# Expert units ordered by tile count, with programs that prepare an equal successor and loop on themselves

## The reference, cut to what matters

```python
_, top2 = jax.lax.top_k(probs, 2)                     # two experts of four for each token
for e in range(e_total):
    member = (top2 == e).any(-1)
    order = jnp.argsort((~member).astype(jnp.int32), axis=-1, stable=True)
    xg = jnp.take_along_axis(x, order[..., None], axis=1)
    q = (xg @ wq[e] + bq[e]).reshape(b, s, h, hd)      # k and v alike
    att = jnp.einsum('bqhd,bkhd->bhqk', q, k) * sm_scale
    att = jnp.where(validg[:, None, None, :], att, -1000000000.0)
    att = jax.nn.softmax(att, axis=-1)
    y = jnp.einsum('bhqk,bkhd->bqhd', att, v).reshape(b, s, d)
    y = y @ wo[e] + bo[e]
    out = out.at[bidx, order].add(wg[..., None] * y)
```

## Time and profile before

| | us |
|---|---|
| median of 3 runs | 4405.09 |
| lowest, highest | 4398.52, 4405.25 |
| the profiled execution | 4440.01 |
| its span, first to last instruction | 4438.2 |
| PE busy | 3516.6 (79%) |
| DVE busy | 2407.3 (54%) |
| ACT busy | 2102.3 (47%) |
| POOL busy | 892.9 (20%) |

### The profile page before, as it was taken

One profiled execution on the slowest core, in us unless ns is written; L12 is line 12 of the kernel. 1 busy time (PEld: TensorE's weight loads), 2 busy tenths in 40 slices (PEclk: granted clock), 3 DMA queues, 4 the chain that ended last, 5 costly groups with the idle time before them and its releaser, 6 DMA issues.

```text
span 4438.2 us, 58078 instructions
## 1 busy us (share of the span) xinstructions
PE 3516.6 (79%) x21592; PEld 1672.6 (38%) x21593; DVE 2407.3 (54%) x3490; ACT 2102.3 (47%) x4547; POOL 892.9 (20%) x686
## 2 busy tenths in 40 slices
PE   4998989757779777797777977779279979788795
PEld 2444435332333333333333333332134435344574
DVE  3664656534366443664436644365276797875523
ACT  1664656425346553464534745347135545454121
POOL 1132422220110002100021000200233423110274
PEclk8998999869789997998989989889679989899898
DMA  4544435330431204312043121420342414123488
GB/s 137 167 147 125 134 105 169 94 79 20 110 91 33 65 20 110 89 33 65 20 115 84 33 66 32 113 73 12 100 116 84 122 55 123 38 61 100 107 202 225
DMA packets 329702, 407.57 MB, mean 92 GB/s; under 512 B 43992, under 2 KB 292120, under 8 KB 321163
## 3 DMA queue, kind: packets, MB, share of 16 engines
q1 hardware_dynamic: 277148, 346.89, 27.7%
q0 software_dynamic: 18432, 35.67, 3.4%
q10 hardware_dynamic: 33664, 19.53, 2.0%
HBM read 234.31 MB, written 158.14 MB: 88 GB/s over the span
## 4 chain that ended last, share of the span: by engine, by line
PE 54%; DVE 21%; issue 8%; DMA 5%; ACT 5%; POOL 3%; ACTq 2%; SPq 2%; another core or an unknown queue 1%; POOLq 0%; DVEq 0%
PE PSUM L768 13%; DVE M L997 13%; PE PSUM L728 10%; PE PSUM L746 10%; PE PSUM L673 6%; PE PSUM L790 3%; PE PSUM L709 2%; ACT P L938 2%; DVE best L1321 2%; DVE XR L1324 2%; ACTq L550 1%; PE PSUM L776 1%; PE PSUM L587 1%; PE PSUM L731 1%
## 5 line engine op out<-in xcount | busy, mean ns | idle before, releaser
L997 DVE TENSOR_REDUCE M<-PSUM 128x1 f32<-128x768 f32 (+7 forms) x1710 | 1715.2, 1037 | 1276.1 <-PE PSUM L728 778.1
L938 ACT ACTIVATE P<-PSUM 128x512 f32<-128x512 f32 (+2 forms) x3520 | 1577.8, 503 | 877.0 <-PE PSUM L746 524.6
L728 PE MATMUL PSUM<-KS,QS 99*128 99x512 bf16 (+3 forms) x3596 | 956.9, 349 | 410.8 <-issue 204.6
L746 PE MATMUL PSUM<-QS,KS 101*128 101x512 bf16 (+2 forms) x3520 | 1077.8, 344 | 108.4 <-ACT P L938 67.7
L768 PE MATMUL PSUM<-P,VA 128*17 128x512 f32 (+3 forms) x7040 | 779.8, 520 | 1.8 <-ACT P L938 0.9
L746 PEld LDWEIGHTS PSUM<-QS,KS 101*128 101x128 bf16 x3520 | 330.5, 99 | 858.8 <-ACT P L938 484.6
L728 PEld LDWEIGHTS PSUM<-KS,QS 99*128 99x128 bf16 x3596 | 312.1, 100 | 853.7 <-DVE M L997 373.9
L639 POOL TENSOR_TENSOR QF<-QF,PH 128x1024 f32<-128x1024 f32 (+2 forms) x98 | 160.3, 1635 | 2115.2 <-ACT PH L893 2077.8
L673 PE MATMUL PSUM<-XT,W 128*128 128x512 f32 (+2 forms) x656 | 313.5, 606 | 7.3 <-ACT P L938 3.8
L768 PEld LDWEIGHTS PSUM<-P,VA 128*17 128x17 f32 x7040 | 135.9, 97 | 239.3 <-issue 203.4
L731 PE MATMUL PSUM<-identb,maskB 128*128 128x128 bf16 x1024 | 218.3, 228 | 0.0
(11 more groups left out here) (189 smaller groups left out, 3121.6 us busy)
## 6 DMA issues: line engine op xcount, KB each, us to landing
qk_d<-PH SPq DMA_DIRECT2D x156, 256.0 KB
xg_d<-GX SPq DMA_DIRECT2D x19, 1152.0 KB, 11.1
yg_d<-GX SPq DMA_DIRECT2D x17, 1152.0 KB
XF<-xg_d SPq DMA_DIRECT2D x18, 1024.0 KB
VA<-n_L_ffn_expert_gate_up_w SPq DMA_DIRECT2D x64, 256.0 KB, 5.8
QS<-qk_d SPq DMA_DIRECT2D x42, 384.0 KB, 5.4
KS<-qk_d SPq DMA_DIRECT2D x42, 384.0 KB, 4.8
QS<-qk_d SPq DMA_DIRECT2D x42, 256.0 KB, 5.8
```

What stands on the lines that cost most here:

```text
L728: mm = e.matmul(slot_heads(s, hb)[:, x, a:b], QS[0:KA, g, h + x, 128 * qt:128 * qt + 128], KS[0:KA, g, h + x, a:b], start=True, stop=not d ...
L746: mm = e.matmul(s[:, 0:q1 - q0], KS[0:KB, g, j, 128 * kt:128 * kt + 128], QS[0:KB, g, j, q0:q1], start=True, stop=not diag, skip_group_che ...
L938: e.activation(P[:, m % NP, 0:q1 - q0], s[:, 0:q1 - q0], ACT.Exp, scale=ly.scale).then_inc(S["act_p"], 1)
L997: e.tensor_reduce(m[:, qt, h:h + hb], v[:, :, 0:kn], AX.X, ALU.max).then_inc(S["dve_a"], 1)
```

## The change

Unit 0 stays first. Units 1 to 15 are sorted on DVE by falling tile count (`order_units`: two rounds of `max` and a `match_replace` on the score 32 x tiles - u), which gives `key` and a new list `sequence` of unit numbers. A program reads from `sequence` which unit it is (u), which it prepares (nu) and whose rows it loads (nu of nu). There are 16 programs: for the first unit one of each nt that prepares at 8 tiles (kinds 1 to 8), for the others one of each nt that prepares at nt tiles (kinds 9 to 16). `key` holds the tile count of unit 0, then 8 + tiles. The register `kind` is loaded at a program's start; at its end the program compares it, and where it is its own kind it goes through a `meet` block of its own (`again`) back to its start. The rows of the second unit are loaded by the first unit's program, no longer in `l0`. The core of the diff:

```diff
-                "bk": [("dve_x", 6)],
+                "bk": [("dve_x", 15)],
-        ev += [(13.0, ("nx", B)), (13.05, ("nv", B)), (13.1, ("fr", B)), (16.1, ("nr", B))]
+        ev += [(13.0, ("nx", B)), (13.05, ("nv", B)), (13.1, ("fr", B))]
...
+    if layer.first:
+        ev.append((-2.0, ("nr", 2)))
...
+        def order_units(e, w, before):
+            later = slice(1, B * E0)
...
+            e.tensor_scalar(count, count, 1.0, 32.0, ALU.max, ALU.mult).then_inc(x, 1)
+            e.tensor_tensor(score, count[:, later], sequencef[:, later], ALU.subtract).then_inc(x, 1)
+            e.max(top[:, 0:8], score).then_inc(x, 1)
+            e.match_replace(left, top[:, 0:8], score, NEG).then_inc(x, 1)
+            e.max(top[:, 8:16], left).then_inc(x, 1)
...
+            e.tensor_scalar(keyf[:, later], tiles, float(NT), None, ALU.add).then_inc(x, 1)
+            e.scalar_tensor_tensor(sequencef[:, later], tiles, 32.0, top[:, 0:n], ALU.mult, ALU.subtract)
...
+                    if i == 3:
+                        w.wait_ge("pe_a", "xt", 2, O.layer.of(2).nch - 1, 1)
+                        e.sem_clear(S["ahead_rows"])
+                    e.dma_start(XF[:, :, :], x_rows(v["block"] if i == 3 else v["block1"]))
...
-        units = {3 * nt + a: unit_order(Unit(nt, PADS[a])) for nt in range(1, NT + 1) for a in range(3)}
+        units = {nt: unit_order(Unit(nt, FIRST, True)) for nt in range(1, NT + 1)}
+        units.update({NT + nt: unit_order(Unit(nt, nt, False)) for nt in range(1, NT + 1)})
...
+            e.dma_start(sequencef[:, :], d["c_iota"][:, 0:B * E0 + 2]).then_inc(S["setup"], 16)
...
+            kinds = [NT + nt for nt in range(NT, 0, -1)] + list(range(NT, 0, -1))
+            def names():
+                if name not in ("sp", "act"):
+                    return None
+                for k, reg in enumerate((this, after, third)):
+                    e.reg_load(reg, sequence[0:1, bass.ds(position() + k, 1)])
...
             with nc.body(label + "tests", valid_engines=on):
-                e.br_cmp(at, B * E0, label + "end", label + "key", "IS_EQ")
-            with nc.body(label + "key", valid_engines=on):
-                kind = e.value_load(key[0:1, bass.ds(unit(), 1)], min_val=kinds[0], max_val=last_kind)
-                e.br(label + f"test{kinds[0]}")
+                e.br_cmp(at, B * E0, label + "end", label + f"test{kinds[0]}", "IS_EQ")
...
                 with nc.body(label + f"program{k}", valid_engines=on):
                     hint = e.mark_branch_hint_location()
-                    u = unit()
-                    section(units[k], {"u": u, "ex": u % E0, "nu": u + 1, ...
+                    v = names()
+                    nc.regs_alu(at, at, 1, op=ALU.add)
+                    e.reg_load(kind, key[0:1, bass.ds(nc.snap(at, min_val=1, max_val=B * E0), 1)])
+                    section(units[k], v)
                     arrive(e, name)
-                    nc.regs_alu(at, at, 1, op=ALU.add)
-                    e.br(label + "tests").branch_hint(hint)
+                    if k > NT:
+                        e.br_cmp(kind, k, label + f"again{k}", label + "tests", "IS_EQ")
+                    else:
+                        e.br(label + "tests").branch_hint(hint)
+                if k > NT:
+                    with nc.body(label + f"again{k}", valid_engines=on):
+                        meet(e, name)
+                        e.br(label + f"program{k}").branch_hint(hint)
```

More of the change, by code:

```diff
@@ L28 @@
 EARLY = 20
-PADS = (3, 6, 8)
+FIRST = NT
 ENGINE_SEMS = ["pe_a", "pe_s", "pe_v", "act_a", "act_p", "act_o", "act_x", "dve_a", "dve_x", "dve_r",
@@ L101, with __init__ @@
 class Unit(Layer):
-    def __init__(self, nt, ahead):
+    def __init__(self, nt, ahead, first):
         Layer.__init__(self, "moe", 1, nt, False, 0.5)
         self.next = Layer("moe", 1, ahead, False, 0.5)
+        self.first = first
     def of(self, i):
@@ L477, in build @@
         base = sb("base", [128, 1])
-        cnt = sb("cnt", [1, B * E0 + 1], I32)
-        keyf = sb("keyf", [1, 3, B * E0 + 1])
-        key = sb("key", [1, B * E0], I32)
+        cnt = sb("cnt", [1, B * E0], I32)
+        key = sb("key", [1, B * E0 + 1], I32)
+        keyf = sb("keyf", [1, B * E0 + 1])
+        sequence = sb("sequence", [1, B * E0 + 2], I32)
+        sequencef = sb("sequencef", [1, B * E0 + 2])
         nfl = sb("nfl", [1, B * E0 + 1])
@@ L1164, in attention_dve @@
                 elif kind == "bk":
[L1165 to L1179, removed]
+                    order_units(e, w, O.at("dve_x", *task) - 15)
@@ L1543, in attention_sp @@
                 elif kind == "nr":
[L1544 to L1547, removed]
+                    if i == 3:
+                        w.wait_ge("pe_a", "xt", 2, O.layer.of(2).nch - 1, 1)
+                        e.sem_clear(S["ahead_rows"])
+                    e.dma_start(XF[:, :, :], x_rows(v["block"] if i == 3 else v["block1"])).then_inc(S["ahead_rows"], 16)
             for name in DMA_SEMS:
@@ L1581, in setup_sp @@
             e.dma_start(rw[:, :, 0:E0], kn_weights(d["L0_ffn_router_w"])).then_inc(S["setup"], 16)
-            n += 16 * 10
+            e.dma_start(sequencef[:, :], d["c_iota"][:, 0:B * E0 + 2]).then_inc(S["setup"], 16)
+            n += 16 * 11
             e.dma_start(QS[96:99, :, :, :].rearrange("p g h n -> p (g h n)"), d["c_rows"]).then_inc(S["setup"], 16)
@@ L1600, in setup_dve @@
             e.memset(mhalf[:, :], -0.5)
-            e.memset(cnt[:, :], 0)
+            e.memset(keyf[:, :], 0.0)
             e.memset(GX[:, 0, 0, :], 0.0).then_inc(S["act_x"], 1)
@@ L1887, in unit_loop, with position @@
             on = [e.engine]
-            at = nc.alloc_registers(f"units_{name}_u", engines=on)
             label = f"units_{name}_"
-            kinds = sorted(units)
+            at, kind, this, after, third = [nc.alloc_registers(label + x, engines=on)
+                                            for x in ("at", "kind", "this", "after", "third")]
+            kinds = [NT + nt for nt in range(NT, 0, -1)] + list(range(NT, 0, -1))
             last_kind = kinds[-1]
-            def unit():
+            def position():
                 return nc.snap(at, min_val=0, max_val=B * E0 - 1)
+            def names():
+                if name not in ("sp", "act"):
+                    return None
+                found = []
+                for k, reg in enumerate((this, after, third)):
+                    e.reg_load(reg, sequence[0:1, bass.ds(position() + k, 1)])
+                    found.append(nc.snap(reg, min_val=0, max_val=B * E0 - 1 + k))
+                u, nu, nnu = found
+                return {"u": u, "ex": u % E0, "nu": nu, "nex": nu % E0, "block1": nu + 1, "block": nnu + 1, "yb": u + 1}
             arrive(e, name)
             nc.regs_mov(at, 0)
+            e.reg_load(kind, key[0:1, 0:1])
             e.addr_align(256, offset=0, max_nops=0)
```

28 lines of the change are left out of this document (26 added, 2 removed), and 2 rows, old and new, of the table ONE_BANK.

## The result

The changed kernel takes 4246.49 us in the median of 4 runs (4240.4 to 4253.64), the kernel before 4401.81 on the same chip (4387.46 to 4405.25, 4 runs): a ratio of 0.9652, interval 0.9633 to 0.9671, or 155 us less. The forecast was 89 less, 4316, and 4275 was the bottom of its range: the sign was right, the size was not.

The account below looks back on a forecast made before the run. PE bounds units of 6 and 7, latencies those of 2, DVE's maxima the tail of 3; gaps hold 163.3 us. Windows -55, gaps -67, loads +29, additions +4 sum to -89: 4316 us, range 4275 to 4378.

Parts of the forecast that it names:

- New order: Order of units worked out from the stores: 6 (preparing 8), 7 four times, 6 three, 3 four, 2 four.
- The step of 0.31 us a squared tile: Windows of 7 and 6: 8.5 us for 27 squared tiles prepared, giving 203.4 for a 7 and 163.3 for a 6.
- 55 more, +17, 172: First unit, 6 preparing 8: 55 squared tiles more add 17 us, giving 172, then 175 with its rows' load.
- The other step: Tail of a 3 preparing 3: fewer DVE maxima and no s1 pass, -23 us of 43, 20 staying.
- if it all shows: Lower bound of 64 us for a 3 preparing 3, against 70 forecast and 76 from the other side.
- the reading of the 0.24 us: Gaps of repeats: 0.24 us in rows 6 taken as evidence against a 4 us fetch for each repeat's branch.
- exit and setup: One load and one memset more in setup, exit to `tests` without a hint: +4 us, between 0 and 5.
- the fetch rival: Loop pays for its fetch, the hint helping no more than in `meet`: 29 us and some more, 4347; chance 0.2.
- the one miss in four: Gaps of repeats: only three of four repeats counted as hits of the branch.
- all of it shows: Register loads at program starts delay the first activation, on which PE waits: 1.8 us a unit, +29 us.
- Small units side by side: Rival: eight small units in a row keep the clock at 0.5, +224 us, kernel 4540; chance 0.05.
- The repeat was taken: Rival: repeat not taken or order wrong, all fifteen transitions cost 12 us, 4400, no change; chance 0.02.

Follow-up runs that it names:

- the kernel before with other sizes: Kernel before with `PADS = (3, 7, 8)` in place of 3, 6, 8, so a 3 ahead of a 7 and a 7 ahead of a 6 prepare 7: 4414.58 us, 0.9932.
- four more loads: Changed kernel with four further reads of `sequence` per unit on SP and on ACT, each used in an address: 4272.32 against 4400.7 us, 0.9709.

## Why the prediction was right or wrong

**New order.** As worked out from the stores: PE's counts are x946, four of x1072, three of x924, four of x272, four of x188.

**Windows of 7 and 6.** The step of 0.31 us a squared tile gave 203.4 for a 7 without the loads; the kernel before with other sizes took 204.8 in the mean of three, the changed kernel, with its loads, 205.9. Both means hold a unit in which PE waited for biases (207.2 and 208.7); the others are 203.5 and 203.6 against 204.4 to 205.9. So the step was right, and what the loads cost here is 1 to 2 us, no more than the same unit varies between runs. For the 6s it gave 163.3, and 161.9 was measured with the loads; a 6 had no row preparing more than 3, and the price came from the 7s.

**The first unit: the price of a size.** 175 forecast, 183.4 measured. The wait for a DMA at its start, on which I put 3, is 0.9 us in that profile. Without it the window is 182.5, where "55 more, +17, 172" had the size: the 0.31 us a squared tile, taken from a 7 that goes from 3 to 6, is too little where a 6 prepares 8. It is some 28 us for 55 there, 0.5 each, and the run that prepares 7 gives the same.

**A unit of 3: the step that failed.** "The projections fall from 32 matmuls to 16, 17.2 to 8.7 us, in part hidden: -4." What they lost was not hidden. The stretch ahead of the tail fell from 52.9 to 42.4 us, -10.5, and the chain of waits spends 5.6 us on them where it spent 14.5. The other step held: the tail of 43 us, for which I had -23 and 20 that stay, fell by 22.9 to 20.4. The rest of the miss is my start from 97, which is the first of the four; their mean is 96.2. That is 7.2 us a unit, 29 in all, of which 26 are the projections and what else lies ahead of the tail. 62.8 is below my bound of 64 for "if it all shows".

**A unit of 2.** I took off 3 us for maxima and 2 to 3 for projections, from 56.1 to 51; it went from 56.3 to 53.1. On the chain of waits the maxima take 2.9 less and the projections 2.5 less, as forecast, and other pieces some 2 more, which I had not reckoned with. With the loads' 1.8, which didn't come, the sum of 52.8 fitted the measured 53.1 by two errors: luck.

**Gaps.** The picture, fetches for branches, was right, and the reading of the 0.24 us in the earlier trace rows as a hit too; the fetch rival (4347) is refuted, and in the 6s and 7s it is the hint that refutes it. Wrong was the one miss in four: none of 11 missed (-9 us). And for the four other transitions I put 12 us each, as if all paid two fetches; only two do (-17).

**The register loads: a right price in the wrong place.** +29 forecast, 1.7 us a unit measured on ACT's queue, 0.1 on the first activation relative to PE. What failed is "all of it shows": the wait it was to lengthen is counted from PE's start, which moved by 0.9 too, and the issues behind it got 0.7 faster. That a delay at that place costs about its full size is shown by four more loads.

**The rivals.** Small units side by side don't hold the clock down: 0.92 to 0.85 in the 3s (0.89 to 0.93 before), 0.69 to 0.74 in the 2s (0.71 to 0.77), 0.81 over all eight: in the mean 0.02 to 0.03 lower than before, and far from 0.5. The repeat was taken 11 times of 11.

**The sum** missed by 66 us. By cause: loads 29 too dear, gaps 26, units of 3 29, exit and setup 3.5, and against these some 22 that the other windows took beyond their own terms, 8 of them in the first unit. The windows' -62 lie within the -95 to -15 that I gave, the loads at the lower end of 0 to 38, the gaps' -93 beyond their -85. The terms' ends would have reached -180; the range was cut at -135, as if three terms couldn't be out in the same direction.

## What to carry to other kernels

Before a term is called hidden in part, cut the window where the work stands and look at the chain of waits there: the 9 us by which the projections shrank were all on it, while in the tail the work of the other engines did stay. An engine's busy time that moves with the window over four sizes is not proof that it sets it. Price a delay at a start from the instruction that waits for it, and against the start of the engine it meets there, not from the queue in which it stands. This loop paid 3 to 5 us for each branch to code that wasn't in place: let equal programs follow each other, and name a large one's start with a hint far ahead. Before an experiment with a doubled instruction is believed, count the instruction in its trace.

## What the runs showed of the hardware that I had not expected

A hint on a branch brought 4 us in programs of 6 and 7 tiles and nothing in those of 2 and 3, which a repeat finds in place without it; I had thought of the two as one thing. How far that goes (which size of program is the last to stay) was not tried. In the kernel before, SP's way back to `tests` took 4.0 us after a 6 and 4.4 after a 7, with a hint; in the run where every program goes back there, with the same hint, the chain has 0.18 after a 7 and 0.41 after a 3. The order of the blocks in memory and the order of the kinds both differ, and which of the two did it was not tried.

A branch to code that is not in place seems to cost more than its own wait: an issue some instructions behind it took 1.80 us instead of 0.42, and in the mean the seven issues of a start took 0.7 less after the change.

Most reads of one number from SBUF into a register take 0.26 to 0.46 us. The first read on every engine takes 0.9 to 1.1 in the five repeats of programs of 7 and 6 tiles, and in no repeat of those of 3 and 2, though the five engines begin to read within 0.3 us of each other in both; why is open. The rows are those of the changed kernel (min, median, max in ns):

```profile
L1932 SPq TENSOR_LOAD <-sequence x48: 261/272/1102, 894.7 to 2868.2; - x48
L1932 ACTq TENSOR_LOAD <-sequence x32: 272/449/1072, 894.2 to 2867.8; - x32
```
